# Loading two steps of edge records at once and storing the sums of four, in the attention layer of a four-layer graph network on Trainium2

## The chip, the cores and the metric

The kernel runs on one core of one Trainium2 chip. The metric is the device time of one execution in microseconds (us), from runs without a profile; lower is better. One further execution was profiled, and every row shown here comes from it. The engines are named as in the profile: PE is TensorE (matrix products; PEld is its weight load), DVE is VectorE, ACT is ScalarE, POOL is GpSimd, SP is SyncE, which here does nothing but issue transfers. "Idle before" is the time in which an engine stood still ahead of an instruction, and behind the arrow stands what ended it; "issue" there means nothing that the profile shows, and "remote" a semaphore event for which the profile found no instruction.

## What is computed

Four graph layers, each followed by an addition of its input and a layer norm. A graph of 12,500 nodes with 64 features and 200,000 edges. The change touches the third layer alone, which in the reference is:

```python
def _forward(x, edge_weights, W_att1, b_att1, W_att2, b_att2, W_lin, b_lin, ..., edge_idx):
    src = edge_idx[0]
    dst = edge_idx[1]
    lin_x = x @ W_lin.T + b_lin
    feat = jnp.concatenate([x[src], edge_weights, x[dst]], axis=1)
    h = jax.nn.relu(feat @ W_att1.T + b_att1)
    scores = (h @ W_att2.T + b_att2)[:, 0]
    m = jax.ops.segment_max(scores, src, num_segments=num_nodes)
    e = jnp.exp(scores - m[src])
    denom = jax.ops.segment_sum(e, src, num_segments=num_nodes)
    alpha = e / denom[src]
    msg = jax.ops.segment_sum(alpha[:, None] * lin_x[dst], src, num_segments=num_nodes)
    ...
```

For every edge, the features of both its ends and 16 edge features go through a small network that gives a score, and the messages of all edges of one source node are summed with softmax weights. A gated update of each node (GRU) follows in a later part of the program.

## The kernel before, in words

**Tiles and steps.** The edges are sorted by source node beforehand and laid out so that each of 128 partitions holds a run of 1568 consecutive edges (`W`). A tile is one column of this layout, 128 edges, one per partition. `edge_layer` runs one layer over these columns; in the third layer (`l = 2`, kind `"gated"`) it takes `G = 7` tiles per step, so there are `STEPS = 224` steps. A step `s` uses slot `u = s % 8` of ring buffers with `RING = 8` slots.

**Buffers.** `slab[:, u]` holds the edge records of the 7 tiles (16 features, a one and the index of the far node, 18 words each). `pair[:, u, g, 0:64]` holds the features of the far node of tile `g`, and `pair[:, u, g, 64:128]` the features of the near node: the seed, which lies in memory only at the first edge of a node's run, and which DVE then copies down the run (`fill`). `message` holds the weighted rows, `kept` the running sums that are stored to `sums`. The profile prints these names with `l_` ahead.

**What each engine does for a step.**

- SP, `load(s)` (lines 1132 to 1138): once `message` of step `s - 8` is done, it issues the transfer of the records (L1135) and of the seeds (L1137) of step `s`; both count on one semaphore, `slab_in[u]`. In the same turn of its loop `save(s - 12)` (L1142) stores the sums of 7 tiles once `kept` of that step is done.
- POOL, `one(s)` (L1096): it waits for `message` of step `s - 8` and for `slab_in[u]`, and then issues seven gathers, one for each tile, which fetch 128 far-node rows each by the indices in `slab`. POOL's software makes the descriptors of these gathers.
- DVE, `fill` (L1203) while it also adds the sums of step `s - 3` (L1317 and the copy of the maxima, L1322), then the dot products with the output weights of step `s - 1` (L1212) and `make_message` of step `s - 2` (L1262).
- PE, `flip` (L1391): eight transposes (seven of `pair`, one of `slab`) once the rows have landed and `fill` is done; `hidden` (L1402, L1406) of step `s - 1`: three groups of products, at the end of each of which DVE is told.
- ACT, `evacuate` (L1481): copies the transposed tiles out of PE's banks into `turned`, for `hidden`; and the exponentials (L1467, L1469).

**What sets the order.** `in_turn` writes out all turns in a row, so each engine has one fixed sequence, and semaphores alone set when it goes on. The loop that is closed through the eight slots is: message of `s - 8` (DVE), load of `s` (SP), gathers of `s` (POOL), transposes, products, scores (PE, ACT, DVE), message of `s`.

## Time and profile before

| | |
|---|---|
| time, median of 3 runs | 15592.24 us (15556.44 to 15619.84) |
| the profiled execution: time | 15569.8 us |
| the profiled execution: span, first to last instruction | 15568.0 us |
| first to last gather of the third layer | 9572.24 to 12352.1 us |
| POOL busy over the span | 57% |
| DVE busy over the span | 38% |
| PE busy over the span | 16% |
| DMA queues' mean share of 16 engines | software queue (POOL's gathers) 8.6%, SP's 7.5% |

No engine is busy throughout, and the program is a row of stages. The third layer's edge loop takes 2780 us, 18% of the span; it is the only stage that the change touches. The shares over the whole span say nothing about it, so the rows below are of that stage.

### The profile page before, as it was taken

What the parts mean: (1) busy time and instruction counts of PE and PEld (TensorE: products, weight loads), DVE (VectorE), ACT (ScalarE), POOL (GpSimd) and SP (SyncE); (2) the same over time, 40 slices, a digit from 0 to 9 for tenths busy, and PEclk for the clock granted to TensorE, in tenths of its full rate; (3) what the DMA queues carried; (4) which work ended last, traced back from release to release, by engine and by line L of the source; (5) the groups of instructions that cost most, each with busy time, mean ns of one, the idle gap of its engine ahead of it and who ended that gap; (6) DMA issues with size and microseconds to landing.
All of it is one profiled execution on the core that took longest, in us unless ns stands there. A gap on an engine that the chain in (4) does not pass through costs nothing. (4 is left out here: it accounts for less than half of the span.)

```text
span 15568.0 us, 59095 instructions
## 1 busy us (share of the span) xinstructions
PE 2433.1 (16%) x11516; PEld 1918.4 (12%) x11516; DVE 5860.0 (38%) x14807; ACT 2267.7 (15%) x3624; POOL 8805.1 (57%) x8546
## 2 busy tenths in 40 slices
PE   0100000333330000000000001444454431000000
PEld 0000000222220000000000000333343331000000
DVE  8511111988862222222111111455455433222223
ACT  0100000333301111111222210111111100111111
POOL 0477777000007777776777776555555412777776
PEclk7555555555555555555555555777777755555555
DMA  4111110000011111111111111222222201211111
GB/s 147 20 14 13 13 13 13 0 0 0 0 34 42 49 49 49 49 47 49 47 47 47 47 47 39 59 64 60 61 65 61 54 6 13 50 47 49 49 49 46
DMA packets 709731, 627.97 MB, mean 40 GB/s; under 512 B 455664, under 2 KB 538761, under 8 KB 708499
## 3 DMA queue, kind: packets, MB, share of 16 engines
q0 software_dynamic: 273056, 240.52, 8.6%
q1 hardware_dynamic: 434608, 372.85, 7.5%
q10 hardware_dynamic: 1728, 11.11, 0.2%
q14 instruction: 252, 2.06, 0.0%
q8 instruction: 87, 1.43, 0.0%
HBM read 319.01 MB, written 304.83 MB: 40 GB/s over the span
## 5 line engine op out<-in xcount | busy, mean ns | idle before, releaser
L1096 POOL DMA_INDIRECT l_rows<-table,l_sources x4704 | 4936.6, 1049 | 1610.6 <-issue 1576.3
L1096 POOL DMA_INDIRECT l_pair<-table,l_slab x1568 | 1497.0, 955 | 1288.1 <-DMA l_pair<-seeds 794.7
L546 POOL DMA_INDIRECT e_rows<-in_rec,base x1568 | 1690.1, 1078 | 482.9 <-issue 481.6
L982 POOL DMA_INDIRECT seeds<-near_seed,seed_at_d x196 | 189.9, 969 | 2534.3 <-POOLq L910 1909.9
L1293 DVE TENSOR_TENSOR_SCAN l_totals<-l_factor,banks 128x510 f32<-128x510 f32 (+3 forms) x672 | 752.6, 1161 | 1912.1 <-ACT banks L1449 1865.7
L1224 DVE TENSOR_TENSOR l_score<-l_rows,base 128x14 f32<-128x14 f32 x224 | 42.7, 191 | 3210.7 <-DMA l_rows<-table,l_sources 3210.7
L1459 ACT COPY l_kept<-l_totals 128x476 f32<-128x476 f32 (+3 forms) x672 | 638.8, 966 | 3714.6 <-issue 2769.6
L1412 PE MATMUL banks<-ident,l_kept 128*65 128x128 f32 (+2 forms) x4 | 1.9, 464 | 7091.9 <-issue 4653.7
L699 PE MATMUL banks<-Z 125*128 125x98 bf16 x3200 | 623.1, 366 | 3012.6 <-DVE Z L682 2976.8
L407 ACT COPY area<-area 128x2048 f32<-128x2048 f32 x342 | 642.1, 1926 | 2939.1 <-DVE area L332 1688.6
L1402 PE MATMUL banks<-w_each,l_turned 128*128 128x288 f32 (+1 forms) x1344 | 667.4, 586 | 1349.3 <-ACT l_turned L1481 950.5
L1412 PEld LDWEIGHTS banks<-ident,l_kept 128*65 128x65 f32 (+2 forms) x4 | 0.7, 170 | 7092.8 <-issue 4654.1
L332 DVE COPY_PREDICATED area<-banks,area 128x2048 f32<-128x2048 int32 x342 | 869.9, 2597 | 5.9
L682 DVE TENSOR_TENSOR Z<-count_j,digit_d 125x2048 bf16<-125x2048 bf16 x200 | 209.6, 1094 | 1722.3 <-remote 1297.5
L699 PEld LDWEIGHTS banks<-Z 125*128 125x128 bf16 x3200 | 455.4, 148 | 3178.0 <-DVE Z L682 3038.8
L323 DVE TENSOR_TENSOR area<-area 128x512 f32<-128x512 f32 (+1 forms) x936 | 797.0, 904 | 37.2 <-ACT area L394 27.3
L1212 DVE SCALAR_TENSOR_TENSOR l_junk<-banks,w_out 128x144 f32<-128x144 f32 x1568 | 407.5, 302 | 992.5 <-remote 627.6
L1406 PEld LDWEIGHTS banks<-w_in,l_turned 128*128 128x128 f32 x3136 | 609.2, 239 | 193.0 <-issue 125.8
L1406 PE MATMUL banks<-w_in,l_turned 128*128 128x144 f32 x3136 | 616.6, 336 | 0.0
L1481 ACT COPY l_turned<-banks 128x512 f32<-128x512 f32 x448 | 248.2, 587 | 2396.5 <-remote 1529.3
L1317 DVE SCALAR_TENSOR_TENSOR l_kept<-l_kept,l_factor,l_message 128x65 f32<-128x65 f32 x1568 | 452.2, 288 | 368.6 <-remote 135.6
L1449 ACT COPY banks<-l_rows 128x476 f32<-128x476 f32 x224 | 196.1, 907 | 1739.5 <-DMA l_rows<-table,l_sources 1739.5
(323 smaller groups left out, 5859.1 us busy)
## 6 DMA issues: line engine op xcount, KB each, us to landing
l_rows<-table,l_sources POOLq DMA_INDIRECT x4704
sums<-l_kept SPq DMA_DIRECT2D x112, 476.0 KB
sums<-l_kept SPq DMA_DIRECT2D x224, 231.0 KB
sums<-l_kept SPq DMA_DIRECT2D x112, 462.0 KB
seeds<-zeros SPq DMA_DIRECT2D x130, 392.0 KB
sums<-l_kept SPq DMA_DIRECT2D x112, 448.0 KB
l_pair<-seeds SPq DMA_DIRECT2D x224, 224.0 KB
e_rows<-in_rec,base POOLq DMA_INDIRECT x1568
```

The costliest lines, as they stand in the source:

```text
L323: ins_ = V.tensor_tensor(to, lo, hi, op)
L332: ins_ = V.copy_predicated(to[i], m, was[1 - i])
L407: AC.copy(to[i], was[i]).then_inc(s["copied"], 1)
L546: GP.indirect_dma_start(e_rows[:, u, g, :], None, A["rec16"], bass.IndirectOffsetOnAxis(e_ids[:, s * G16 + g:s * G16 + g + 1], 0)).then_in ...
L699: mm = PE.matmul(ps["ds".index(k)][:, 0:NB], hot[0][0:EP, i % 2, :, c], hot[1][0:EP, i % 2, 0:NB, c], start=s == 0 and c == 0, stop=True, ...
L1096: GP.indirect_dma_start(pair[:, u, g, 0:D] if gated else rows[:, u, g, :], None, table[l], bass.IndirectOffsetOnAxis(at, 0)).then_inc(rows ...
L1212: V.scalar_tensor_tensor(junk[:, g % 2, :], hidden_at(g), 0.0, extra["w_out"][:], ALU.max, ALU.mult, accum_out=score[:, u, g:g + 1]).then_ ...
L1293: V.tensor_tensor_scan(flat(totals[:, s % 2, h, 0:n, :]), flat(factor[:, s % 2, 0:n, :]), flat(fresh[s % 2][h][:, 0:n, :]), 0.0, ALU.mult, ...
L1317: V.scalar_tensor_tensor(kept[:, u, g, 0:M], old, factor[:, u, g:g + 1], message[:, u, g, :], ALU.mult, ALU.add).then_inc(kp.sem, 1)
L1402: PE.matmul(ps[4 + i][:, 0:n * H1], turned[:, u % 2, G * P:], extra["w_edge"][:, a:a + n, :].rearrange("p g h -> p (g h)"), start=True, st ...
L1406: mm = PE.matmul(hidden_at(g), turned[:, u % 2, g * P:(g + 1) * P], extra["w_in"][:], start=False, stop=True, skip_group_check=True)
L1459: AC.copy(kept[:, s % KR, :, a:a + n], totals[:, s % 2, h, 0:n, 1:G + 1].rearrange("p f g -> p g f")).then_inc(S["kept"].sem, 1)
```

## The change

In the third layer alone:

- SP loads in even steps only, two steps at once: one transfer of the records and one of the seeds for 14 tiles (`PAIR = 2`), counted on one of four semaphores `slab_in[u // 2]`. It waits for `message` of step `s + 1 - 8 = s - 7`, since the transfer overwrites the slots of two steps.
- SP stores the sums of four steps, 28 tiles, at once (`PER = 4`), in turn `s + 8` where `s` is the last of the four, and no longer those of 7 tiles in turn `s + 12`. The last four steps are stored as two, one and one.
- POOL waits for `slab_in` in even steps only, and for `message` of step `s - 8` in each, as before.
- DVE waits for a store only at every fourth step, for the store of the same half of the `kept` ring.

The other three layers have `PER = 1` and the same instructions as before.

```diff
+                PER = 4 if gated else 1
                 KR = RING if gated else 4
+                SETS = KR // PER
+                cuts = list(range(0, STEPS, PER)) + ([STEPS - 2, STEPS - 1] if PER > 2 else []) + [STEPS]
+                save_sets = list(zip(cuts, cuts[1:]))
+                set_of = lambda s: s // PER % SETS
...
-                            pool.wait_ge(*slab_in[u].done(r))
+                            if u % PAIR == 0:
+                                pool.wait_ge(*slab_in[u // PAIR].done(r))
...
                     def load(s, r, u):
+                        if s % PAIR:
+                            return
                         if later(s, RING):
-                            sp.wait_ge(*done("message", s - RING))
-                        sp.dma_start(slab[:, u, 0:G * RE], recs[:, bass.ds(s * (G * RE), G * RE)]
-                                     ).then_inc(slab_in[u].sem, 16)
-                        sp.dma_start(pair[:, u, :, D:2 * D], seeds[:, bass.ds(s * G, G), :]
-                                     ).then_inc(slab_in[u].sem, 16)
+                            sp.wait_ge(*done("message", s + PAIR - 1 - RING))
+                        n = PAIR * G
+                        sp.dma_start(slab[:, u:u + PAIR, 0:G * RE],
+                                     recs[:, s * G * RE:(s * G + n) * RE].rearrange("p (s w) -> p s w", s=PAIR)
+                                     ).then_inc(slab_in[u // PAIR].sem, 16)
+                        sp.dma_start(pair[:, u:u + PAIR, :, D:2 * D].rearrange("p s g w -> p (s g) w"),
+                                     seeds[:, s * G:s * G + n, :]).then_inc(slab_in[u // PAIR].sem, 16)
 
                     def save(s, r, u):
-                        sp.wait_ge(*done("kept", s))
-                        sp.dma_start(to[:, bass.ds(s * G, G), :],
-                                     kept[:, s % KR, :, :]).then_inc(saved[s % KR].sem, 16)
-
-                    in_turn(STEPS, RING, [(0, load), (12, save)] if gated else [(0, save)])
+                        for a, b in save_sets:
+                            if b == s + 1:
+                                sp.wait_ge(*done("kept", s))
+                                sp.dma_start(to[:, a * G:b * G, :], kept[:, a % KR:a % KR + b - a, :, :]
+                                             .rearrange("p s g w -> p (s g) w")).then_inc(saved[set_of(a)].sem, 16)
+
+                    in_turn(STEPS, RING, [(0, load), (8, save)] if gated else [(0, save)])
...
-                                if later(s, RING):
-                                    dve.wait_ge(*saved[u].done(r - 1))
+                                if s % PER == 0 and later(s, KR):
+                                    dve.wait_ge(*saved[set_of(s)].done(len(saves_by(s)) - 1))
```

What stands in a row on SP in the third layer once all its kinds of transfer are under way, before (`l_slab<-rec_s` is the records' load, `l_pair<-seeds` the seeds', `sums<-l_kept` the store; the last numbers are partitions and elements):

```order
L1135 DMA l_slab<-rec_s 128x126 [waits message]
L1137 DMA l_pair<-seeds 128x7x64
L1142 DMA sums<-l_kept 128x462 [waits kept]
L1135 DMA l_slab<-rec_s 128x126 [waits message]
L1137 DMA l_pair<-seeds 128x7x64
L1142 DMA sums<-l_kept 128x462 [waits kept]
```

And now, for the same two steps and two more:

```order
L1145 DMA l_slab<-rec_s 128x2x126 [waits message]
L1148 DMA l_pair<-seeds 128x14x64
L1145 DMA l_slab<-rec_s 128x2x126 [waits message]
L1148 DMA l_pair<-seeds 128x14x64
L1155 DMA sums<-l_kept 128x1848 [waits kept]
```

Three transfers a step became five for four steps; the store moved from behind every load to behind every second one.

What stands on POOL where the ring is used for the second time (steps 8 to 10), before; each row with a wait is the first gather of a step:

```order
L1096 DMA l_pair<-table,l_slab 128x64 [waits slab_in0,message]
L1096 DMA l_pair<-table,l_slab 128x64 x6
L1096 DMA l_pair<-table,l_slab 128x64 [waits slab_in1,message]
L1096 DMA l_pair<-table,l_slab 128x64 x6
L1096 DMA l_pair<-table,l_slab 128x64 [waits slab_in2,message]
```

And now:

```order
L1103 DMA l_pair<-table,l_slab 128x64 [waits slab_in0,message]
L1103 DMA l_pair<-table,l_slab 128x64 x6
L1103 DMA l_pair<-table,l_slab 128x64 [waits message]
L1103 DMA l_pair<-table,l_slab 128x64 x6
L1103 DMA l_pair<-table,l_slab 128x64 [waits slab_in1,message]
```

No gather moved; the wait for a load stands ahead of each second step only, and the load behind it needs the message of one step later than the gather itself does.

## Rows read from the trace of the kernel before

**Rows 1.** Waits, all engines, 9560 to 12400 us: us, times, longest

```profile
ACT l_turned L1481 <- remote: 1529.3, 134, 61.9
...
POOL l_pair L1096 <- DMA l_pair<-seeds: 794.7, 98, 23.5
```

**Rows 2.** Lines, POOL in the loop: count | busy, mean ns | idle before, releasers

```profile
L1096 POOL DMA_INDIRECT l_pair<-table,l_slab x1568 | 1497.0, 955 | 1288.1 <-DMA l_pair<-seeds 794.7 <-issue 493.4
```

**Rows 3.** Timeline of POOL, loop start: start, us, instruction [idle before <-releaser]

```profile
9572.24 0.96 POOL L1096 DMA_INDIRECT l_pair<-table,l_slab  x1 [5.21 <-issue]
...
9640.93 0.94 POOL L1096 DMA_INDIRECT l_pair<-table,l_slab  x1 [0.30 <-issue]
9665.34 0.94 POOL L1096 DMA_INDIRECT l_pair<-table,l_slab  x1 [23.46 <-DMA l_pair<-seeds]
```

**Rows 4.** Timelines of PE, ACT and DVE in that same first run

```profile
9592.64 0.27 PE L1391 MATMUL banks<-ident,l_slab 128*128 128x128 f32 x1
...
9646.96 0.58 ACT L1481 COPY l_turned<-banks 128x512 f32<-128x512 f32 x1 [61.95 <-remote]
...
9601.46 0.31 DVE L1212 SCALAR_TENSOR_TENSOR l_junk<-banks,w_out 128x144 f32<-128x144 f32 x1 [23.57 <-remote]
...
9618.26 0.31 DVE L1212 SCALAR_TENSOR_TENSOR l_junk<-banks,w_out 128x144 f32<-128x144 f32 x1 [16.02 <-issue]
...
9635.06 0.31 DVE L1212 SCALAR_TENSOR_TENSOR l_junk<-banks,w_out 128x144 f32<-128x144 f32 x1 [16.26 <-remote]
```

**Rows 5.** Timeline of SP, start of the loop: issue of the loads

```profile
9576.92 0.69 SPq L1137 DMA_DIRECT2D l_pair<-seeds  x1
...
9579.02 0.69 SPq L1137 DMA_DIRECT2D l_pair<-seeds  x1
...
9661.12 0.33 SPq L1135 DMA_DIRECT2D l_slab<-rec_s  x1
```

**Rows 6.** Timeline of POOL, 12200 to 12345 us: gathers after a stop

```profile
12204.10 0.94 POOL L1096 DMA_INDIRECT l_pair<-table,l_slab  x1 [12.51 <-DMA l_pair<-seeds]
...
12230.04 1.00 POOL L1096 DMA_INDIRECT l_pair<-table,l_slab  x1 [8.77 <-DMA l_pair<-seeds]
...
12269.24 0.94 POOL L1096 DMA_INDIRECT l_pair<-table,l_slab  x1 [12.51 <-DMA l_pair<-seeds]
...
12294.91 0.94 POOL L1096 DMA_INDIRECT l_pair<-table,l_slab  x1 [8.50 <-DMA l_pair<-seeds]
```

**Rows 7.** Timeline of SP in that stretch: record loads, each just behind a message

```profile
12225.20 0.32 SPq L1135 DMA_DIRECT2D l_slab<-rec_s  x1
...
12231.78 0.32 SPq L1135 DMA_DIRECT2D l_slab<-rec_s  x1
...
12238.44 0.32 SPq L1135 DMA_DIRECT2D l_slab<-rec_s  x1
...
12265.12 0.32 SPq L1135 DMA_DIRECT2D l_slab<-rec_s  x1
...
12272.76 0.32 SPq L1135 DMA_DIRECT2D l_slab<-rec_s  x1
```

**Rows 8.** Timelines after the last gather: POOL's last, then DVE's messages

```profile
12351.19 0.94 POOL L1096 DMA_INDIRECT l_pair<-table,l_slab  x1 [0.30 <-issue]
...
12367.44 0.62 DVE L1262 TENSOR_TENSOR l_message<-l_pair,l_message 128x448 f32<-128x448 f32 x1
...
12387.14 0.62 DVE L1262 TENSOR_TENSOR l_message<-l_pair,l_message 128x448 f32<-128x448 f32 x1
```

**Rows 9.** Waits of SP's own queue, 9560 to 12400 us

```profile
SPq L1135 <- DVE l_message L1262: 1747.7, 130, 69.5
...
SPq L1142 <- DVE l_kept L1322: 48.3, 7, 12.9
```

More of the change, by code:

```diff
@@ L1012, in edge_layer @@
                 buf = lambda n, shape, dt=F32: sbt(ctx, name(n), shape, dt)
+                PER = 4 if gated else 1
                 KR = RING if gated else 4
+                SETS = KR // PER
+                cuts = list(range(0, STEPS, PER)) + ([STEPS - 2, STEPS - 1] if PER > 2 else []) + [STEPS]
+                save_sets = list(zip(cuts, cuts[1:]))
+                set_of = lambda s: s // PER % SETS
+                saves_by = lambda s: [b for a, b in save_sets if set_of(a) == set_of(s) and b <= s]
                 kept = buf("kept", [P, KR, G, R])
@@ L1053, in edge_layer @@
                 rounds = lambda u: STEPS // RING - 1 + (u < STEPS % RING)
-                slab_in = ring("slab_in", 32) if gated else None
+                PAIR = 2
+                slab_in = [again(f"slab_in{i}", 32, STEPS // RING) for i in range(RING // PAIR)] if gated else None
                 rows_in = ring("rows_in", 16 * G)
-                saved = [again(f"saved{u}", 16, STEPS // KR + (u < STEPS % KR)) for u in range(KR)]
-                saves = lambda u: STEPS // KR - 1 + (u < STEPS % KR)
+                saved = [again(f"saved{h}", 16, sum(set_of(a) == h for a, _ in save_sets)) for h in range(SETS)]
                 S = dict(kept=st("kept", G + 1 if gated else 3 if soft else 2), factor=st("factor", 1))
@@ L1101, in edge_gpsimd @@
                     in_turn(STEPS, RING, [(0, one)])
-                    for u in range(KR):
-                        pool.wait_ge(*saved[u].done(saves(u)))
+                    for h in range(SETS):
+                        pool.wait_ge(*saved[h].done(sum(set_of(a) == h for a, _ in save_sets) - 1))
                     pool.sem_inc(gathers_begun, 1)
@@ L1187, in one @@
                             if g == 0:
-                                dve.wait_ge(*slab_in[u].done(r))
+                                dve.wait_ge(*slab_in[u // PAIR].done(r))
                                 dve.wait_ge(*done("runs", s))
@@ L1452, in keep @@
                     def keep(s, r, u):
-                        if later(s, KR):
-                            act.wait_ge(*saved[s % KR].done(s // KR - 1))
+                        if s % PER == 0 and later(s, KR):
+                            act.wait_ge(*saved[set_of(s)].done(len(saves_by(s)) - 1))
                         if soft:
```

## The prediction

> **What bounds the kernel now.** The change touches one stage, the edge loop of the third layer, 9572 to 12352 us. I read the waits of that stretch first, then the timelines of POOL and SP side by side.
>
> POOL is the engine to follow. Its 1568 gathers take 1497.0 us with 493.4 us of short pauses between them: 1990.4 / 224 = 8.89 us for the seven gathers of a step. The rest of its idle time is 794.7 us in 98 waits for a load of seeds [rows 2]. The first of them, behind the first eight steps, is 23.46 us [rows 3]; the other 97 have a mean of 771.2 / 97 = 7.95 us. So from 9665 to 12352 us, 216 steps, POOL works in runs of 216 / 97 = 2.2 steps, with a stop of 8 us behind each. A step takes 2687 / 216 = 12.44 us; 8.89 of it are gathers and 3.6 are stops.
>
> Why does POOL stop for a load? Not because loads are slow as such. SP issues one as soon as a message has freed its slot (1747.7 us of its waiting is for L1262, [rows 9]), and the first gather of that step starts some 4.2 us later: 9661.12 to 9665.34, 12265.12 to 12269.24 [rows 3, 5, 6, 7]. POOL runs eight steps ahead and stops because the messages don't come. The question is why they don't, while PE, ACT and DVE are mostly idle.
>
> The first run answers it. POOL gathers without pause from 9572.24 to 9641.9 [rows 3]. The rows of the first steps are long there. PE's last transpose of step 1 is over at 9592.9 by its row, and the copy that takes it out of PE's bank starts on ACT at 9646.96, 5 us behind POOL's last gather, after 61.95 us of standing still; three dot products that wait for PE start 16.8 us apart, at 9601.46, 9618.26 and 9635.06 [rows 4]. Over the stage ACT loses 1529.3 us in this way [rows 1]. So what PE hands on doesn't arrive, or hardly, while POOL gathers in a long run, and flows again when it stops. The later runs show the same: loads, each just behind a message, at 12225.20, 12231.78 and 12238.44, the last two 1.7 and 8.4 us into the run that started at 12230.04; then none for 26.7 us, until 12265.12, which is 8.4 us behind that run's end (12269.24 less its stop of 12.51) [rows 6, 7]. Without gathers the chain of engines is quick: behind the last gather the messages at 12367.44 and 12387.14, with two between, are 19.70 / 3 = 6.6 us apart [rows 8].
>
> **A sum for the stage.** A step needs 6.6 us in which its hand-overs flow. These flow in a stop, and in the first 8 to 9 us of a run, but not in the first few us of a stop. Call what a run and its stop give beyond the stop itself c. With runs of n steps, n x 6.6 = stop + c. Before: 2.23 x 6.6 = 14.7 = 7.95 + c, so c = 6.8 us. The time of a step is then 8.89 + 6.6 - 6.8 / n. With n = 2.23 that is 12.44, as observed. It is gathers and hand-overs one after the other, less an overlap of 6.8 us that each run gives once: **few long runs are bad, many short ones are good**.
>
> **The change, part by part.**
>
> *Half as many loads, twice as large.* Removed: 224 issues of 0.3 to 0.45 us on SP, which waits most of its time [rows 9]; worth nothing. The price is the longer way from message to gather. Low bound: 4.2 us as now, if the larger transfer hides in the same fixed time. High bound: queued loads follow each other by 9579.02 - 9576.92 = 2.1 us [rows 5], so 6.3 us. I take 5.5, nearer the high end, because the bytes double.
>
> *The wait is one message later.* The load of steps e and e + 1 needs the message of e - 7, where step e alone needed e - 8. That is a message more, 6.6 us, if hand-overs flow. It isn't simply added: in that time the chain works. It decides the length of the runs. Take a stop in which the message that frees a pair comes; 5.5 us later a run starts. The next message comes 6.6 us behind the first, 1.1 us into the run, and the one after that 7.7 us into the run. A message 8.4 us into a run still came through before [rows 6, 7]. With it the next pair is free; its load lands at 7.7 + 5.5 = 13 us, before the first pair's gathers end at 2 x 8.89 = 17.8 us. So the run goes on, for four steps. At its end the last message is that of e - 5, and the next load, of e + 4 and e + 5, needs that of e - 3: two are missing, and both come in the stop. The stop is then 8.4 + 6.6 + 5.5 = 20.5 us, and by the sum 4 x 6.6 - 6.8 = 19.6 us. The two agree.
>
> *Length of a step.* n = 4: 8.89 + 6.6 - 1.7 = 13.8 us. n = 3: 13.2. n = 2: 12.1. Some third messages will miss and leave a run of two, so I take a mean n of 3.5: 13.55. In long runs a hand-over now and then gets through (one in 16.8 us, [rows 4]); a run of 35 us has one more of these than one of 20, worth the part of a step that follows it, about a fifth of 6.6 us, 1.3 / 3.5 = 0.3 at most; I take 0.15. **13.4 us a step, +0.96 x 216 = +207 us.**
>
> *The stores.* One transfer stands where there were four, of the same bytes. The wait for `kept` stands behind a load in SP's queue, and ahead of the next one. The next load needs message 4k + 5, the store needs kept 4k + 3, and DVE makes that one turn earlier. So the store is never last; 48.3 us of such waits exist now at lag 12 [rows 9], and I expect the same or less. What is queued behind it is only that next load, and POOL behind the load. DVE waits for the store of four steps ago, at least four turns old (50 us): hidden. Bounds: 0, and for a store in the load's way once in four steps at 2.1 us, 54 x 2.1 = +113 us. I take 0, since a message's time, 6.6 us, lies between them.
>
> *Ends of the stage.* The first load is twice as large, before any gather: +1 to +2 us. The drain behind the last gather, 6.6 us for each message still out, stays. Together 0.
>
> Sum: 15569.8 + 207 = 15777 us against the profiled execution, which is 22 us below the median of the runs; against the median, 15592 + 207 = **15800 us**, 1.3% slower.
>
> **The page that speaks against this.** What the rows show is that POOL waits 4.2 us from a load's issue to its gather, once for each stop [rows 3, 5]. The Trainium skill, DMA: Bandwidth & Descriptors, section Rules for kernel authors, says that many small transfers should be coalesced into one large one, and gives a fixed cost of about 2 us for each. By that rule the 112 loads that fall away, each a pair of transfers side by side, save some 112 x 2 = 224 us (an estimate from the page's figure), and the time would be about 15370 us. By the rows they save nothing, since POOL stops for a message, and not for the load's fixed cost.
>
> **Rivals.**
>
> 1. *Runs stay short.* The message 7.7 us into a run is held back, so that the pair isn't free and POOL stops after two steps. For it: 8.4 us is close to the edge, and most runs now have two steps, not three. Against it: the first message is earlier in the run than now. Then n is 2 to 2.5, 12.1 to 12.8 us a step, -70 to +70 us: 15520 to 15660, middle 15590.
>
> 2. *A stop costs a fixed time and fewer stops are a gain* (faster, the other side). If hand-overs are held back not by the gathers but by the mixture of gathers with SP's transfers, or if the chain can catch up in any stop, then each run of two or four steps ends in one stop of 7.95 + 1.3 us, as now. With 60 stops for 97: 97 x 7.95 - 60 x 9.25 = 771 - 555 = 216 us less, 15375 us. This is the case in which the page above is right. It decides itself at whether a stop behind four steps stays under 4 x 12.44 - 4 x 8.89 = 14.2 us. Against it: runs of three are followed by stops of 12.5 us, runs of two by 8.5 to 8.8 [rows 6], and in the first run, 50 us without any transfer of SP's, hand-overs stood still as well.
>
> 3. *Even longer runs.* With more than four steps in a run, or a store in the way of the load, the step is 8.89 + 6.6 - 6.8 / 6 = 14.4 us: +415 us, 16000 us.
>
> **How the numbers follow.** Forecast with n of 3 to 4 (13.0 to 13.8 us a step, +120 to +295 us: 15710 to 15890): 0.58. Rival 1: 0.22. Rival 2: 0.14. Rival 3: 0.06. The range reaches from the middle of rival 1's lower half, 15550, to 15930, which takes in the bound of a store in the way for one half; about 0.2 is left out, most of it rival 2. Half a per cent, 78 us, is about what a measurement of this kernel can tell from no change. Slower by more than that: the forecast, rival 3 and a little of rival 1, 0.65. Within: 0.20. Faster: rival 2 and a little of rival 1, 0.15.
>
> **What would show it.** In the profile after: POOL's waits for seeds, 50 to 70 instead of 98, but 950 to 1000 us in all instead of 794.7; stops of about 20 us behind runs of four steps (the time from stop to stop some 55 us); ACT's wait that ends in "remote" above 1529 us; the gathers' own mean unchanged at 955 ns. Loads 5 to 6 us ahead of the gather they release. Wrong would be: fewer waits and a smaller sum (rival 2), or some 98 waits again with runs of two (rival 1). If stops are shorter than 14 us behind runs of four, the sum for the stage falls, and with it the claim that gathers hold up the hand-overs. All other stages should keep their times.

## The result, and the profile after

| | before | after |
|---|---|---|
| time, median of 4 runs each | 15589.38 us (15556.44 to 15619.84) | 15723.75 us (15715.74 to 15728.32) |
| the profiled execution: time | 15569.8 us | 15723.3 us |
| first to last gather of the third layer | 9572.24 to 12352.1 us | 9562.54 to 12504.2 us |
| a step, behind the first run of eight | 12.44 us | 13.15 us |

The changed kernel takes 1.0082 of the time before, with an interval of 1.0065 to 1.0099: 134 us slower. In the profiled executions the difference is 153.5 us. The last message of the stage starts 154.5 us later (12552.1 us for 12397.6), and the stage's first gather 9.7 us earlier, so all of the loss is in the third layer's loop. A step takes (12504.2 - 9663.4) / 216 = 13.15 us.

The waits of all engines, 9560 to 12600 us, of the kernel after (us in all, times, longest one); its first two rows answer to [rows 1]:

```profile
ACT l_turned L1494 <- remote: 1484.2, 110, 61.3
POOL l_pair L1103 <- DMA l_pair<-seeds: 959.9, 56, 31.3
...
POOL l_pair L1103 <- issue: 489.0, 1507, 18.3
```

And POOL's gathers in the view by line, which answers to [rows 2]:

```profile
L1103 POOL DMA_INDIRECT l_pair<-table,l_slab x1568 | 1497.3, 955 | 1450.4 <-DMA l_pair<-seeds 959.9 <-issue 489.0 <-DVE l_message L1275 1.5
```

The gathers themselves are unchanged: 955 ns each. POOL waits for a load 56 times instead of 98, and 165.2 us longer in all (959.9 against 794.7). That is the whole loss, with the 9.7 us by which the stage began earlier. One stop of 18.3 us is put down to "issue", and two of the 56 rows are pauses of 0.30 us.

What a cycle looks like is seen in three timelines of the kernel after. POOL, 11415 to 11560 us, the gathers behind a stop (between them stand only gathers with the usual pause of 0.3 us):

```profile
11415.64 0.94 POOL L1103 DMA_INDIRECT l_pair<-table,l_slab  x1 [16.72 <-DMA l_pair<-seeds]
...
11468.09 0.96 POOL L1103 DMA_INDIRECT l_pair<-table,l_slab  x1 [17.39 <-DMA l_pair<-seeds]
...
11520.49 0.94 POOL L1103 DMA_INDIRECT l_pair<-table,l_slab  x1 [17.16 <-DMA l_pair<-seeds]
```

DVE, 11475 to 11530 us: the messages (L1275), and the dot product (L1225) that the first message of the stop had waited for:

```profile
11475.68 0.62 DVE L1275 TENSOR_TENSOR l_message<-l_pair,l_message 128x448 f32<-128x448 f32 x1
...
11507.75 0.31 DVE L1225 SCALAR_TENSOR_TENSOR l_junk<-banks,w_out 128x144 f32<-128x144 f32 x1 [17.73 <-remote]
...
11508.21 0.62 DVE L1275 TENSOR_TENSOR l_message<-l_pair,l_message 128x448 f32<-128x448 f32 x1
...
11514.78 0.62 DVE L1275 TENSOR_TENSOR l_message<-l_pair,l_message 128x448 f32<-128x448 f32 x1
...
11521.33 0.61 DVE L1275 TENSOR_TENSOR l_message<-l_pair,l_message 128x448 f32<-128x448 f32 x1
```

SP, 11490 to 11530 us, its loads and one store:

```profile
11493.70 0.33 SPq L1155 DMA_DIRECT2D sums<-l_kept  x1
11515.42 0.36 SPq L1145 DMA_DIRECT2D l_slab<-rec_s  x1
11515.83 0.47 SPq L1148 DMA_DIRECT2D l_pair<-seeds  x1
11528.50 0.36 SPq L1145 DMA_DIRECT2D l_slab<-rec_s  x1
```

POOL works in runs of exactly four steps (52.40 us from stop to stop, of which 35.2 are gathers), with a stop of 17 us behind each. The run that began at 11468.09 ends at 11520.49 - 17.16 = 11503.33. In it a message comes at 11475.68, and then none until 11508.21. It stands directly behind two dot products, the first of which had waited 17.73 us; the profile puts this wait down to "remote", and in the program these dot products wait for PE's products of `hidden`. The next one, 6.6 us later, frees the pair of slots; SP issues the load at 11515.42, 0.02 us behind it, and the first gather starts 5.07 us after that. The whole stage is made of this: 54 runs of four steps, the first stop 31.3 us, the other 53 of 17.7 us in the mean (959.9 - 31.3 - 6.1 of the wait ahead of the first gather - 0.6 + 18.3 = 940.2 us).

Waits of SP's own queue in the same stretch, which answer to [rows 9]:

```profile
SPq L1145 <- DVE l_message L1275: 1402.7, 94, 89.2
SPq L1155 <- remote: 1006.0, 46, 29.3
```

SP now also waits long at the store, 1006.0 us for events put down to "remote" and 204.1 us for `kept` itself, where it waited 48.3 us before. No load is late for it: the store at 11493.70 is out 21.7 us before the load behind it, and of all stores that a load follows none is out less than 7.8 us before it.

### The profile page after: what moved, and what is told of

It reads as the page before. It is cut to its first block and busy times, and to the rows that moved or that the text cites. A ratio compares the mean times of both kernels' runs of the same rounds, so it can differ in the third digit from the quotient of the medians.

```text
span 15721.6 us, 58591 instructions
## 1 busy us (share of the span) xinstructions
PE 2405.2 (15%) x11516; PEld 1893.2 (12%) x11516; DVE 5842.6 (37%) x14807; ACT 2269.6 (14%) x3624; POOL 8809.3 (56%) x8546
## 5 line engine op out<-in xcount | busy, mean ns | idle before, releaser
L1103 POOL DMA_INDIRECT l_pair<-table,l_slab x1568 | 1497.3, 955 | 1450.4 <-DMA l_pair<-seeds 959.9
L1225 DVE SCALAR_TENSOR_TENSOR l_junk<-banks,w_out 128x144 f32<-128x144 f32 x1568 | 398.7, 301 | 844.3 <-remote 732.2
L1494 ACT COPY l_turned<-banks 128x512 f32<-128x512 f32 x448 | 245.9, 588 | 2476.1 <-remote 1484.2
L1415 PEld LDWEIGHTS banks<-w_each,l_turned 128*128 128x128 f32 x1344 | 263.0, 237 | 1600.6 <-ACT l_turned L1494 848.7
```

The costliest lines, as they stand in the source:

```text
L1103: GP.indirect_dma_start(pair[:, u, g, 0:D] if gated else rows[:, u, g, :], None, table[l], bass.IndirectOffsetOnAxis(at, 0)).then_inc(rows ...
L1225: V.scalar_tensor_tensor(junk[:, g % 2, :], hidden_at(g), 0.0, extra["w_out"][:], ALU.max, ALU.mult, accum_out=score[:, u, g:g + 1]).then_ ...
L1415: PE.matmul(ps[4 + i][:, 0:n * H1], turned[:, u % 2, G * P:], extra["w_edge"][:, a:a + n, :].rearrange("p g h -> p (g h)"), start=True, st ...
```

## The experiments

**A condition that the runs brought to light.** The runs were made on several chips, and the kernel before does not take the same time on all of them: 15557.74 us and 15561.41 us on two, about as above, but 12367.58 us and 12358.08 us on two others. The difference touches the very thing on which the prediction rests. On the quick chips the third layer's traces show no such hold-up of what PE hands on. So the first seven kernels below, which fell on the quick chips, could not test what they were made for; they show what the parts of the change are worth without the hold-up. I give them first, in short, and then the five that ran on chips with it.

The hold-up isn't peculiar to the third layer. In an early stage DVE makes one-hot matrices `Z` for PE while POOL gathers `e_rows`, and makes more of them later, without gathers. The view of one tile (duration in ns: shortest/median/longest, then first and last start), of the kernel before on a chip with the hold-up:

```profile
L682 DVE TENSOR_TENSOR Z<-count_j,digit_d x200: 957/1086/1252, 572.5 to 3243.4; 125x2048 bf16<-125x2048 bf16 x100
L682 DVE TENSOR_TENSOR Z<-count_j,digit_s x200: 954/1086/1251, 3252.4 to 4308.5; 125x2048 bf16<-125x2048 bf16 x100
```

And the same of `stores_only`, on a chip without it:

```profile
L682 DVE TENSOR_TENSOR Z<-count_j,digit_d x200: 952/1086/1249, 572.5 to 1518.2; 125x2048 bf16<-125x2048 bf16 x100
L682 DVE TENSOR_TENSOR Z<-count_j,digit_s x200: 954/1086/1255, 1527.2 to 2585.5; 125x2048 bf16<-125x2048 bf16 x100
```

The instructions take 1086 ns on both chips. The gathers of `e_rows` end at 2708.3 us on the first chip. Until then, 102 of the first 200 instructions are done in 2138 us, 21 us each; the other 98 follow in 535 us, 5.5 us each, and the second 200 take 1056 us, 5.3 us each. On the quick chip the gathers go on to 2874.2 us, so all 400 stand beside them, and the two halves take 946 and 1058 us. So the product is equally fast; what is slow, beside POOL's gathers and on some chips only, is the way from one engine to the next. SP's stores `rec_s<-e_rows` go out in the same stretch as these gathers, so this stage alone doesn't tell the two apart.

### Without the hold-up: the parts of the change

`loads_only` keeps the double loads and undoes the store:

```diff
-                PER = 4 if gated else 1
+                PER = 1
...
-                    in_turn(STEPS, RING, [(0, load), (8, save)] if gated else [(0, save)])
+                    in_turn(STEPS, RING, [(0, load), (12, save)] if gated else [(0, save)])
```

> Of the change, the loads of two steps at once alone; every step's sums are stored by themselves, 12 turns late, as before. Theory (a load that frees two steps makes POOL's runs four steps long, and long runs hold up the hand-overs of PE): all of the loss is here, 134 us, 15710 to 15740 us, with some 54 stops of 17 to 18 us. Rival (the larger, later stores are in the way of the loads or of the gathers): at least half of the loss is gone, 15590 to 15650 us.

Measured: 12360.84 us, 0.9995 of the kernel before on that chip (0.9986 to 1.0005).

`stores_only` keeps the store of four steps and undoes the double loads:

```diff
-                PAIR = 2
+                PAIR = 1
```

> Of the change, the stores of four steps' sums at once alone (8 turns late); every step is loaded by itself, as before. Theory: no difference from before, 15575 to 15610 us, runs of 2.2 steps and about 98 stops of 8 us. Rival (the stores carry the loss): 15650 us or more.

Measured: 12365.25 us, 0.9996 (0.9986 to 1.0005). Its waits of ACT in the stage, 7400 to 9420 us, and POOL's gathers by the page:

```profile
ACT l_turned L1494 <- PE banks L1404: 1669.9, 300, 18.1
```

```profile
L1103 POOL DMA_INDIRECT l_pair<-table,l_slab x1568 | 1500.8, 957 | 483.0 <-issue 469.6
```

ACT has no wait that ends in "remote" here, where there were 1529.3 us [rows 1]. POOL waits for no load but the first and is the bound: (1500.8 + 483.0) / 224 = 8.86 us a step.

`pair_wait_single` is the kernel before with nothing changed but the wait: SP waits once for the message of `s + 1 - 8` and then issues the four old transfers of two steps.

```diff
-                        if later(s, RING):
-                            sp.wait_ge(*done("message", s - RING))
+                        if s % 2 == 0 and later(s, RING):
+                            sp.wait_ge(*done("message", s + 1 - RING))
...
+                    def load_two(s, r, u):
+                        if s % 2 == 0:
+                            load(s, r, u)
+                            load(s + 1, r, u + 1)
...
-                    in_turn(STEPS, RING, [(0, load), (12, save)] if gated else [(0, save)])
+                    in_turn(STEPS, RING, [(0, load_two), (12, save)] if gated else [(0, save)])
```

> Four transfers of the old size for two steps, issued together once the message of the second of the two old steps is done; stores as before. It has the coarse grain of the change without its larger transfers. Theory: runs of four steps again, as long as the changed kernel to within 30 us, 15695 to 15755 us; somewhat less than it, since the first step's load lands sooner. Rival (the size of the transfers costs: the landing takes longer): near before, 15570 to 15620 us.

Measured: 12363.58 us, 0.9996 (0.9986 to 1.0006).

`pool_paced` is the kernel before with POOL tied to the parts of `hidden`, so that its gathers come evenly:

```diff
+                            if gated and later(s, RING) and g in (0, 3, 4, 5):
+                                back, part = {0: (7, 3), 3: (6, 1), 4: (6, 2), 5: (6, 3)}[g]
+                                pool.wait_ge(*S["hidden"].part(s - back, part))
```

> The kernel before, in whose third layer POOL waits four times in a step for a group of hidden products that PE has finished (before gather 0 for the last of step s-7, before gathers 3, 4 and 5 for the three of step s-6). A run then ends soon after a hand-over of PE's is held up, and goes on as soon as it flows. Theory (gathers and hand-overs take turns, each run gives some 7 us of overlap, so short runs are good): shorter runs, 1 to 1.6 steps, 11.0 to 12.0 us a step for 12.44, 100 to 300 us faster than before. Rival (what counts is how far POOL runs ahead, or what a stop costs each time): more waits and a shorter lead, slower than before by 50 us or more.

Measured: 12367.34 us, 1.0002 (0.9992 to 1.0011).

`pool_lead7` lets POOL run seven steps ahead of the messages instead of eight:

```diff
+                            if later(s, RING - 1):
+                                pool.wait_ge(*done(read_last, s - RING + 1))
```

> The kernel before, in whose third layer POOL also waits for the message of step s-7, not only of s-8; its load was issued a message earlier, so the load's way of 4.2 us from issue to gather is off POOL's path. Theory (stops exist because the chain needs time without gathers): nearly nothing is gained, runs of two steps with stops of 6 to 8 us, 12.0 to 12.6 us a step, -90 to +40 us. Rival (a stop costs the way of its load, so fewer or hidden loads are a gain): 97 stops x 4.2 us = 400 us faster.

Measured: 12357.77 us, 1.0000 (0.9991 to 1.0010).

What follows from these five is one thing: where the chain of engines keeps up with POOL, neither half as many loads, nor a quarter of the stores, nor a later or coarser wait, nor a tighter lead changes the time by more than 0.1%. The reasons for the loss aren't tested by them. The rule that spoke for the change (the Trainium skill, DMA: Bandwidth & Descriptors, Rules for kernel authors) says to coalesce many small transfers and names 64 KB as the size under which one pays mostly overhead. The two loads of a step are 128x126 and 128x448 words, 64.5 and 229 KB, so the one is at that size and the other well above it. By the runs, POOL waits for no load here but the first, and 112 fewer of them save 6.7 us in the medians, which is inside the interval.

### Without the hold-up: the chain by itself

`one_gather` issues one gather a step instead of seven. It leaves out the fetching of the rows of six tiles in seven.

```diff
-                        for g in range(G):
+                        for g in range(1 if gated else G):
...
-                                                  bass.IndirectOffsetOnAxis(at, 0)).then_inc(rows_in[u].sem, 16)
+                                                  bass.IndirectOffsetOnAxis(at, 0)).then_inc(rows_in[u].sem, 16 * G if gated else 16)
```

> The kernel before with one gather in a step of the third layer for seven, so the rows of six tiles of each step are never fetched and the third layer's sums are not the reference's; loads, stores and the work of PE, ACT and DVE are unchanged (one clearing of the buffer is added, under 10 us). POOL never works for more than 1.3 us in a row. Theory (POOL's gathers hold up what PE hands on): the chain runs freely, 6.6 us a step, 224 x (12.4 - 6.6) = 1300 us less, about 14290 us, and ACT's waits that end in an event of no known instruction all but go. Rival (SP's transfers or the chain itself hold up the hand-overs): those waits stay, the step stays over 8.5 us, 14700 us or more.

Measured: 11864.13 us in one run, 494 us below the kernel before on that chip. The messages go from 7438.9 to 8912.0 us, 6.6 us apart. Its waits of the stage:

```profile
POOL l_pair L1096 <- DMA l_pair<-seeds: 1207.9, 218, 12.3
ACT l_turned L1482 <- PE banks L1392: 893.4, 225, 18.9
```

So the chain's own pace is 6.6 us a step, the same as in the drain of the slower chip [rows 8], and this term of the sum holds on both.

`pool_memset` has one gather as well, and puts six clears of a spare tile on POOL in place of the six others, to tell POOL's work from its gathers:

```diff
+                    def fill_time(s, r, u):
+                        for g in range(G - 1):
+                            n = s * (G - 1) + g
+                            if n >= 2:
+                                pool.wait_ge(padded.sem, n - 1)
+                            GP.memset(pad[:, n % 2, :], 0.0).then_inc(padded.sem, 1)
```

> As the kernel with one gather in a step, and behind it six clearings of a buffer of 128 x 1100 words on POOL, about 1 us each, so POOL is busy and makes no descriptors. Rows of six tiles are never fetched. Theory A (it is the making and running of gathers that holds up PE's hand-overs): no hold-up, the step is POOL's own time or 6.6 us, whichever is more, and ACT's waits that end in an event of no known instruction are under 300 us. Theory B (any work of POOL holds them up): those waits are near 1500 us as before, the step near 12 us.

Measured: 12830.28 us in one run, 966 us above `one_gather`. That isn't the hold-up that I was after. By their rows DVE's instructions became long. First `one_gather`, its lines of DVE, 7430 to 8900 us (busy, mean ns of one):

```profile
L1263 DVE TENSOR_TENSOR l_message<-l_pair,l_message 128x448 f32<-128x448 f32 x221 | 137.5, 622 | 0.0
...
L1323 DVE COPY l_kept<-l_best 128x7 f32<-128x7 f32 x220 | 38.1, 173 | 0.0
```

Then `pool_memset`, the same view:

```profile
L1333 DVE COPY l_kept<-l_best 128x7 f32<-128x7 f32 x131 | 670.9, 5121 | 0.0
L1273 DVE TENSOR_TENSOR l_message<-l_pair,l_message 128x448 f32<-128x448 f32 x132 | 609.2, 4615 | 0.0
```

By the means, a copy of seven elements a partition goes from 173 to 5121 ns and the message's product from 622 to 4615 ns. The timelines of one step, 7980 to 8010 us, show that only one of them is held up by itself. DVE:

```profile
7982.78 0.29 DVE L1328 SCALAR_TENSOR_TENSOR l_kept<-l_kept,l_factor,l_message 128x65 f32<-128x65 f32 x1
...
7983.12 5.37 DVE L1333 COPY l_kept<-l_best 128x7 f32<-128x7 f32 x1
...
7983.64 4.85 DVE L1273 TENSOR_TENSOR l_message<-l_pair,l_message 128x448 f32<-128x448 f32 x1
```

POOL:

```profile
7982.65 5.81 POOL L1107 MEMSET l_pad<- 128x1100 f32 x6
```

The copy starts beside the clears and ends at 7988.49, as soon as the last of them has (7988.46). The message's product behind it ends in that same moment (7988.49), so it only stood in line behind the copy. The sum at 7982.78, which also reads two tiles of SBUF, ran beside a clear in its usual 0.29 us. This is another effect, between DVE's copy and POOL's clears, and the run says nothing on gathers. It is inconclusive for the question and stands under the surprises below.

### With the hold-up: the changed kernel once more, and a slower ACT

`changed_again` is the changed kernel without an edit, so that the next two have it beside them.

> The changed kernel itself, beside the kernel before, on the chip that this run is given. If PE's hand-overs are held up there while POOL gathers (the kernel before then takes some 15590 us), the theory expects 134 us more again. If they aren't (the kernel before took 12360 us on two other chips), POOL's gathers bound the third layer with no stop at all, at 8.9 us a step, and the change is worth nothing: within 15 us of the kernel before. Rival (the coarser, later loads cost by themselves, hold-up or not): at least 60 us more than before.

Measured: 15723.19 us, 1.0106 (1.0089 to 1.0123) of the kernel before on that chip, which takes 15557.74 us. Its waits of the stage:

```profile
ACT l_turned L1494 <- remote: 1622.5, 123, 61.6
POOL l_pair L1103 <- DMA l_pair<-seeds: 929.3, 58, 31.8
```

The result stands, and so do the runs of four steps: 53 of them in this trace, and two of two. From one chip to the other ACT's "remote" wait goes from 1484.2 to 1622.5 us at the same time of the kernel, so this sum is no measure of the loss.

`act_slow_before` and `act_slow_after` add four copies of a spare tile to ACT in each step, ahead of `evacuate`, in the kernel before and in the changed one:

```diff
+                        def slow(s, r, u):
+                            for _ in range(4):
+                                slowed.link(act, AC.copy(pad[:], pad[:]))
...
-                        in_turn(STEPS, RING, [(0, carry_runs), (3, weight), (1, evacuate)])
+                        in_turn(STEPS, RING, [(0, carry_runs), (3, weight), (1, slow), (1, evacuate)])
```

> The kernel before with four copies of 128 x 2048 words added on ACT in every step of the third layer, ahead of the copy out of PE's banks, 7.7 us a step by the 1926 ns of such a copy in the trace. The chain of PE, ACT and DVE then takes longer than POOL's seven gathers, and POOL has to stop for a message in every step, hold-up or not. Both theories: 13 to 15 us a step, the third layer 900 to 1400 us longer than its 1980 us where nothing is held up.

Measured: 15626.93 us, 1.0048 (1.0032 to 1.0064). The added work by the view by line, and what is left of the waits of [rows 1]:

```profile
L1492 ACT COPY l_pad<-l_pad 128x2048 f32<-128x2048 f32 x896 | 1700.9, 1898 | 21.3
```

```profile
POOL l_pair L1097 <- DMA l_pair<-seeds: 837.6, 99, 21.8
ACT l_turned L1484 <- remote: 706.1, 123, 53.9
```

> The changed kernel with the same four added copies on ACT. Theory (the loss of the change came only from gathers and hand-overs keeping each other waiting): where nothing is held up, POOL stops for messages as often as the slow chain asks, but its rows are ready steps ahead all the same, so this takes as long as the kernel before with the same copies, within 20 us. Rival (a load that needs the message of one step later, and frees two steps at once, costs wherever POOL waits for messages): longer by 60 us or more.

Measured: 15829.39 us, 1.0176 (1.0159 to 1.0193). Its wait for loads:

```profile
POOL l_pair L1104 <- DMA l_pair<-seeds: 1060.2, 80, 32.4
```

The expectations were written for a chain that a slower ACT makes the bound, which holds where nothing is held up. Here it didn't, and the expected 13 to 15 us a step were missed (12.6 us in `act_slow_before`): 1700.9 us of work on an engine in the chain cost 69 us. 823 us of it went into ACT's own "remote" wait (1529.3 to 706.1 us, the two on different chips). What the pair does show: the change costs 15829.39 - 15626.93 = 202 us with ACT slowed and 165 us without. It costs no less where ACT is busy for 69% of the stage than where it is for 11%. That is more than the 60 us that the expectation gave to its rival, but that sentence, like the theory's 20 us, was about a chain that bounds the stage, and decides nothing here. In the trace 48 runs have two steps and 30 have four, and still the sum is 1060.2 us, for 837.6. The mean stop behind a run of two is 8.3 us and behind one of four 21.3 us.

### With the hold-up: the wait alone

`pair_wait_again` is `pair_wait_single` on a chip with the hold-up: transfers and stores as before, only the wait for two messages at once.

> Once more the kernel before with four transfers of the old size for two steps, issued together behind the message of the second of the two old steps, stores as before. Where hand-overs are held up: theory (the coarse wait alone makes the runs four steps long), as slow as the changed kernel to within 30 us, 100 to 165 us slower than before, runs of four steps; rival (the double size of the transfers, or the stores, carry the loss), less than 50 us slower. Where nothing is held up: no difference.

Measured: 15780.66 us, 1.0135 (1.0105 to 1.0165) of the kernel before on that chip (15561.41 us): 219 us slower, which is more than the 100 to 165 us expected, and 57 us more than the changed kernel on another chip. The wait for loads in the stage, and POOL's timeline, 12225 to 12345 us:

```profile
POOL l_pair L1096 <- DMA l_pair<-seeds: 1040.2, 58, 30.4
```

```profile
12230.22 0.95 POOL L1096 DMA_INDIRECT l_pair<-table,l_slab  x1 [20.79 <-DMA l_pair<-seeds]
...
12286.94 0.95 POOL L1096 DMA_INDIRECT l_pair<-table,l_slab  x1 [21.87 <-DMA l_pair<-seeds]
...
12342.88 0.95 POOL L1096 DMA_INDIRECT l_pair<-table,l_slab  x1 [21.03 <-DMA l_pair<-seeds]
```

DVE's messages around the second of these stops, and the first load behind them on SP:

```profile
12273.98 0.62 DVE L1267 TENSOR_TENSOR l_message<-l_pair,l_message 128x448 f32<-128x448 f32 x1
...
12282.24 0.62 DVE L1267 TENSOR_TENSOR l_message<-l_pair,l_message 128x448 f32<-128x448 f32 x1
```

```profile
12282.89 0.32 SPq L1135 DMA_DIRECT2D l_slab<-rec_s  x1
```

This decides it: the coarser wait alone makes the runs of four steps (52 of them, and four of two) and a loss at least as large. Neither the size of the loads nor the stores is needed for it. The changed kernel, which adds the double transfers and the larger stores, even comes out better than this one, 134 to 165 us of loss against 219; which of the two additions does it isn't shown. From the load's issue to the gather it is 4.05 us here and 5.07 us there (4.1 and 5.3 in the mean over all stops), so the larger transfer is slower by 1 us, nearly as assumed. But the first message of the stop is over 9.5 us behind the run's end here (12274.60 - 12265.07), and 5.5 us there. The stops shown are longer than the mean. In the mean of the stops in which two messages come it is 8.1 us here (42 of 52) and 5.8 us there (47 of 53). Why the chain has come further by the end of a run in the changed kernel isn't shown; the mean stops behind four steps are 19.0 and 17.7 us.

### With the hold-up: shorter runs

If few long runs are bad and many short ones good, POOL must be tied close to the chain. `pool_close` is the kernel before with two more waits on POOL: the first gather of step `s` waits for PE's products of step `s - 2`, and the fifth for ACT's copies of step `s - 1`.

```diff
+                            if gated and s >= 2 and g == 0:
+                                pool.wait_ge(*S["hidden"].done(s - 2))
+                            if gated and s >= 2 and g == 4:
+                                pool.wait_ge(*S["turned"].done(s - 1))
```

> The kernel before, in whose third layer POOL keeps close to the chain: ahead of gather 0 of step s it waits for PE's hidden products of step s-2, and ahead of gather 4 for ACT's copy of the transposes of step s-1. Where hand-overs are held up while POOL gathers, POOL then pauses within some 5 us of the first one that is held up, for the 2 to 3 us until it arrives and the copy is done, in place of finishing two or three steps. Theory (overlap of some 7 us a run, so many short runs are good): runs of 4 to 11 gathers, 10.5 to 11.8 us a step for 12.44, 130 to 400 us faster than before. Rival (what counts is the lead of eight steps, or the number of stops): slower than before. Where nothing is held up (the kernel before takes some 12360 us): within 0 to 150 us slower, as the waits have little slack.

Measured: **15183.74 us** (15176.1 to 15186.99), 0.9754 of the kernel before on that chip (0.9725 to 0.9783): 378 us faster, and the best kernel on a chip with the hold-up. It wasn't run on one without. POOL's gathers by line and in the view of the tile:

```profile
L1100 POOL DMA_INDIRECT l_pair<-table,l_slab x1568 | 1509.5, 963 | 917.3 <-issue 512.5 <-PE banks L1410 247.7 <-ACT l_turned L1485 63.0
```

```profile
L1100 POOL DMA_INDIRECT l_pair<-table,l_slab x1568: 938/944/1363, 9569.4 to 11990.1; - x196
```

POOL's timeline, 10285 to 10360 us, gathers behind a stop of over 2 us:

```profile
10286.37 0.99 POOL L1100 DMA_INDIRECT l_pair<-table,l_slab  x1 [2.98 <-PE banks L1410]
...
10307.87 1.00 POOL L1100 DMA_INDIRECT l_pair<-table,l_slab  x1 [3.34 <-remote]
...
10329.49 0.94 POOL L1100 DMA_INDIRECT l_pair<-table,l_slab  x1 [3.81 <-DVE l_message L1266]
...
10350.55 0.94 POOL L1100 DMA_INDIRECT l_pair<-table,l_slab  x1 [2.60 <-DVE l_message L1266]
```

And ACT's "remote" wait, 9550 to 12010 us:

```profile
ACT l_turned L1485 <- remote: 94.0, 28, 14.4
```

POOL stands still more often, 147 times besides what is put down to "issue", but for 917.3 - 512.5 = 404.8 us instead of 794.7, and ACT's wait that was 1529.3 us [rows 1] is 94.0. A step takes 2421.6 / 224 = 10.81 us. The stage's last gather ends at 11991.0 instead of 12352.1 us, and the drain behind it takes 13.1 us instead of 45.5 (last message at 12004.1), since POOL is only two steps ahead. The kernel changes two things at once, the length of the runs and how far POOL runs ahead; no run tells them apart, and 32 us of the gain are the shorter drain.

## Why the prediction was right, and where it was off

**The formula, at four lengths of run.** A step was said to take 8.89 + 6.6 - 6.8 / n us, with c = 6.8 worked out at n = 2.2.

| kernel | steps in a run, n | step by the formula | step measured | mean stop | c = n x 6.6 - stop |
|---|---|---|---|---|---|
| `pool_close` | 1.5 | 11.0 us | 10.81 us | 2.75 us | 7.3 us |
| before | 2.2 | 12.44 us (fitted) | 12.44 us | 7.95 us | 6.8 us |
| `pair_wait_again` | 3.9 | 13.7 us | 13.50 us | 18.4 us | 7.1 us |
| after | 4 | 13.8 us | 13.15 us | 17.7 us | 8.7 us |

Direction and order are right at both ends, between kernels. Within them c can be read more finely, from the gathers behind a stop of over 2 us. In the kernel before, 9 runs have one step, with a mean stop of 7.9 us, 51 have two, with 5.8 us, and 33 have three, with 12.4 us. So c is 7.4 us for runs of two and of three, and below zero for a single step; the fitted 6.8 us is a mixture, and the stops of 8.5 to 8.8 us behind two steps in [rows 6] were no typical ones. `pair_wait_again` has 26.4 - 19.0 = 7.4 us behind its runs of four as well. The changed kernel alone stands apart, with 8.7 us, and 9.2 us in `changed_again`.

In `pool_close` the agreement is one of means only. Its runs of 3, 7, 11 and 14 gathers (23, 14, 23 and 81 of them) have stops of 3.1, 2.2, 2.8 and 3.3 us, which hardly grow with the run.

- **What bounds the kernel.** Right for the chips on which the kernel was measured, with a limit that the prediction did not know: elsewhere the same program runs 3.2 ms quicker, POOL's gathers are the bound at 8.86 us a step, and parts of the change give 0.9995 and 0.9996. The prediction took the hold-up for a property of gathers; it is one of gathers on some chips.
- **The wait is one message later, so runs have four steps.** Right, and shown to be the cause by `pair_wait_again`. All 54 runs had four. Forecast were 3.5 in the mean, because some third messages would miss; none did. In the cycle shown they came 1.5 and 8.0 us into the run (by their ends, 11521.94 and 11528.48 less 11520.49; forecast 1.1 and 7.7).
- **The stop behind a run of four: the term that failed in size.** Forecast were 20.5 us, as 8.4 to the first message, 6.6 to the second and 5.5 to the gather, and 19.6 by the sum. Measured are 17.7, in the cycle shown 5.5 + 6.6 + 5.1 = 17.2. The 8.4 us was taken over from a run of three steps [rows 6, 7], and is also the mean of such runs. In the changed kernel it is 5.8 us in the mean, and 5.2 us in `changed_again`. I had allowed 0.15 us a step for one more hand-over in a long run (the bound written beside it, 1.3 / 3.5, is 0.37 and not 0.3); the term is off by (8.7 - 6.8) / 4 = 0.48. The length of the run doesn't explain it: `pair_wait_again`, whose runs are as long, has 8.1 us, near the forecast. What brings the chain further in the changed kernel stays open.
- **The sum.** By steps: the formula at n = 4 gives 13.8; less 0.48 for c; less 0.10 because the gathers with their pauses took (1497.3 + 489.0 - 18.3) / 224 = 8.79 us instead of 8.89; less 17.7 / 216 = 0.08, one stop fewer than runs. That is 13.14, and 13.15 was measured. As c was taken from the measured stop, this closes the account and tests nothing. Nor did the gathers get quicker: of the 493.4 us put down to "issue" before, 49 us behind the first gather are 34 pauses of over 0.6 us, short stops that the prediction counted as gathers, and after, 16 us besides the one of 18.3. The forecast of 13.4 was nearer than these errors let expect, because n of 3.5 instead of 4 hid half of the error in c. That part is luck. In all 134 us instead of 207, and the time of 15723.75 lies inside the part of the range given for the forecast alone (15710 to 15890).
- **The load's way to the gather.** 5.5 us forecast, 5.1 measured, and 4.05 for two pairs of the old size. **The stores at nothing:** nothing speaks against it. That SP would wait at them for 48.3 us or less was wrong (1006.0 and 204.1 us), but every store is out before the load behind it could go; `stores_only` shows no cost either, though only without the hold-up.
- **What would show it.** 50 to 70 waits, 950 to 1000 us in all: 56 and 959.9. Unchanged gathers: 955 ns. Stops of 20 us every 55: 17.7 every 52.4 in the cycle shown. One was wrong: ACT's wait that ends in "remote" was to rise above 1529.3 us and fell to 1484.2 (and was 1622.5 on the other chip). What ACT waits for is put down to one of several releasers, and this sum moves by 138 us while the time doesn't.

**The rivals.** Runs stay short: no, though two runs of two steps occur in `changed_again`, and 48 of them once ACT is slowed. A stop costs a fixed time, so that fewer are a gain (15375 us): it decided itself at 14.2 us behind four steps, and those stops are 17.7, 17.2, 19.0 and 21.3 us in the mean in four traces. `pool_close`, with half as many stops again and 378 us less, speaks against it from the other side. By the trace the 112 loads that fell away saved nothing, since what POOL waited for was a message. Longer runs than four: none.

**What stays open.** Why PE's hand-overs to ACT and DVE stand still beside gathers, and why on some chips only. No kernel with fewer gathers ran on a chip with the hold-up: `one_gather`, made for that, fell on a quick one. That it is the gathers rests on the traces, on the `Z` stage and on `pool_close`. `loads_only` and `stores_only` weren't run on a chip with the hold-up, nor the changed kernel on one without, so that the sizes of the parts (134 to 165 us against 219 for the wait alone) are known only together; 134, 165 and 219 us are also from different chips. `pool_paced` and `pool_lead7`, the milder ways to shorten the runs, are untried where they could matter.

## What to carry to other kernels

When two kinds of work hinder each other, ask of each change what it does to the length of the runs in which they alternate. A coarser grain of prefetch frees POOL less often and for longer, and may lose more than the transfers it saves. Before a transfer is made larger, look at what its wait ends with: here it was a message from the far end of the ring, and tying POOL closer to the consumers gave 2.5% on one chip with the hold-up, where loading ahead in larger pieces lost 0.8 to 1.1%. And compare with the kernel before on the same chip, since the mechanism that is tested may be absent on the next.

## What the runs showed of the hardware that was not expected

- The same program takes 15.56 ms on two chips and 12.36 ms on two others. The product that makes `Z` takes 1086 ns on both kinds and a gather of `l_pair` 955 to 957 ns in the mean; what differs is above all how long hand-overs take beside POOL's gathers. The gathers of the other layers (`l_rows`) aren't quite equal: 1049 ns in the mean in `before`, 945 ns in `stores_only`.
- Four copies a step on ACT, 1700.9 us in all, cost 69 us in a stage of 2780 us, with ACT in the chain of engines. Most of them fit into time in which ACT stood still anyway (1529.3 us of "remote" waits without them, 706.1 us with them).
- POOL's clears of SBUF hold up a copy on DVE: 173 ns in the mean without them, 5121 ns with them, and in the step shown 5.37 us, until the last of six clears in a row is over. The Trainium skill (SBUF — State Buffer, Who interferes with whom) says that DVE and GpSimd share a pair of ports and block each other. For the copy the trace agrees; it waits there for more than one of the clears, which take 1.03 us each. It says also that an instruction of DVE's with two inputs in SBUF isn't hindered by one of GpSimd's that only writes. The trace agrees: the sums of L1328 keep 0.29 us beside a clear, and the message's product, long by its record (4615 ns in the mean), only stands in line behind the copy and ends with it. No kernel with seven gathers shows the effect: there the product keeps its 621 ns.
